# Prologue of an attention and mixture-of-experts kernel, written out per engine: constants in order of use, first key parts on VectorE

## What is computed

```python
x = x + xattn(layernorm(x), ctx, mask, mask, Wq, bq, Wk, bk, Wv, bv)
    # q, k, v = W @ . + b ; dot = q.k / 4 ; dot = mask*dot - (1-mask)*1e6
    # amap = softmax(dot) * mask ; out = amap.v
x = x + ffn(layernorm(x), gate_w, w1, w2)
    # top 2 of 8 experts: silu(x.w1g) * (x.w1u), then w2, weighted sum
```

## Time and profile before

| what | value |
|---|---|
| median of 3 runs | 975.49 us (974.23 to 975.64) |
| the profiled execution's own time | 971.9 us |
| its span, first to last instruction | 970.1 us |
| mean granted clock of PE | 0.937 of full speed |
| PE busy | 820.0 us (85%) |
| DVE, ACT, POOL busy | 547.9, 316.5, 377.2 us |

### The profile page before, as it was taken

The page is one execution under the profiler, slowest core; times in us unless marked ns, Lnnn a source line. Parts: engine busy times, 40 slices in busy tenths (PEclk is TensorE's granted clock), DMA queues, the critical chain, the costliest instruction groups (busy, mean ns, idle before and its releaser), DMA issues. The chain is left out here.

```text
span 970.1 us, 12844 instructions
## 1 busy us (share of the span) xinstructions
PE 820.0 (85%) x3737; PEld 366.6 (38%) x3738; DVE 547.9 (56%) x1055; ACT 316.5 (33%) x615; POOL 377.2 (39%) x396
## 2 busy tenths in 40 slices
PE   2078999999988998999899986159999999999994
PEld 1022323333333332333333322135555555555552
DVE  3186878788878877878788852403223232323322
ACT  0003556455545655555566675000000000000000
POOL 5643445457545754755474232401111111111111
PEclk9577999899999999999999998569999999999998
DMA  4553656566756856646664423322535365352332
GB/s 118 173 166 110 190 171 193 182 201 195 224 164 185 254 168 189 219 146 184 185 185 139 134 81 120 130 66 55 150 58 146 64 152 141 68 150 59 65 57 40
DMA packets 83567, 137.69 MB, mean 142 GB/s; under 512 B 13880, under 2 KB 39800, under 8 KB 83520
## 3 DMA queue, kind: packets, MB, share of 16 engines
q1 hardware_dynamic: 67792, 107.97, 36.7%
q0 software_dynamic: 7744, 17.86, 9.4%
q10 hardware_dynamic: 7984, 11.28, 4.0%
HBM read 77.34 MB, written 59.36 MB: 141 GB/s over the span
## 5 line engine op out<-in xcount | busy, mean ns | idle before, releaser
L731 DVE TENSOR_REDUCE mx<-tile 128x2 f32<-128x1024 f32 x256 | 309.0, 1217 | 67.8 <-PE tile L1005 64.8
L629 ACT ACTIVATE pr<-sc 128x512 f32<-128x512 f32 x512 | 268.8, 602 | 212.4 <-PE sc L992 209.5
L1005 PE MATMUL tile<-qk 97*128 97x512 bf16 x512 | 160.6, 397 | 43.8 <-DMA qk<-mrow_d 22.3
L1305 POOL DMA_INDIRECT out_dram<-y,ids x36 | 56.1, 1558 | 282.5 <-DVE ids L1230 278.4
L992 PE MATMUL sc<-qk 100*128 100x512 bf16 x512 | 156.2, 386 | 5.0 <-ACT pr L629 3.4
L1021 PE MATMUL pvb<-pr,vp 128*32 128x512 f32 x1024 | 141.3, 625 | 0.0
L1355 PE MATMUL dp<-wring,at 128*128 (+1 forms) x216 | 102.2, 609 | 13.4 <-DVE at L1240 13.4
L1285 ACT ACTIVATE sg<-gp 128x352 f32<-128x352 f32 x36 | 16.7, 463 | 291.7 <-PE up L1334 291.7
L1005 PEld LDWEIGHTS tile<-qk 97*128 97x128 bf16 x512 | 36.6, 98 | 182.5 <-DVE mx L731 75.9
L554 POOL TENSOR_SCALAR parts<-qkf 128x512 bf16<-128x512 f32 x32 | 48.3, 1511 | 140.5 <-DVE qkf L827 139.4
L1334 PE MATMUL gp<-wring,xtile 128*128 x288 | 94.0, 470 | 2.1 <-DVE meta L1221 2.1
(11 more groups left out here) (120 smaller groups left out, 742.2 us busy)
## 6 DMA issues: line engine op xcount, KB each, us to landing
qk<-stack_d SPq DMA_DIRECT2D x32, 768.0 KB
stack_d<-parts SPq DMA_DIRECT2D x32, 384.0 KB, 2.6
wring<-w_dram SPq DMA_DIRECT2D x32, 352.0 KB, 7.0
xl<-routed_d ACTq DMA_DIRECT2D x38, 257.0 KB, 2.7
stack_d<-parts SPq DMA_DIRECT2D x32, 256.0 KB, 2.9
pv_d<-ov SPq DMA_DIRECT2D x32, 256.0 KB, 3.5
xin<-x_dram SPq DMA_DIRECT2D x16, 256.0 KB, 5.8
cin<-ctxt_dram SPq DMA_DIRECT2D x8, 512.0 KB, 6.2
```

The costliest lines, as they stand in the source:

```text
L629: nc.scalar.activation(pr[s % 2][:, j, :], sc[(32 * u + 4 * s + j) % NSC][:, :], ACT.Exp, scale=SCALE).then_inc(exped.sem, 1)
L731: dve.tensor_reduce(mx[:, half(w), 2 * j:2 * j + 2], t[:, :, :], X, ALU.max, negate=True).then_inc(drained.sem, 1)
L1005: last = nc.tensor.matmul(t[:, i, :], qs[half(w)][0:RAW_ROWS, h, c * P:c * P + P], ks[half(w)][0:RAW_ROWS, h, :], start=True, stop=True)
L1305: pool.indirect_dma_start(out, bass.IndirectOffsetOnAxis(ap=ids[:, k, :], axis=0), y[:, k, :], None, compute_op=ALU.add).then_inc(y_added, 16)
```

## The change

Each engine's loop now starts at step -1; what steps -5 to -2 did is written out ahead of it.

- ACT issues `io`, `wq`, `bq`, `wk`, `bk` and `mask` first, with semaphores of their own (`io_in`, `wq_in`, `wk_in`, `mask_in`), and then the other seven.
- POOL sets the ones of half 0, waits for `io` alone, makes the deviations of two units, sets the ones of half 1, and makes the first query parts, two more deviations and the second query parts. It no longer makes the first key parts.
- DVE makes the first key parts itself in `key_parts`: a reduction with the maximum over groups of one element, a subtraction, such a reduction, a subtraction. It takes the statistics of two units before it normalises both; the copies of `idf` and `utf`, which need all the constants, come after the key parts.
- PE waits for `wq` or `wk` before a projection and for `const_made` and the ones only before the first raw scores.
- SP writes `mrow_d` before the query parts and does not wait for it until `stack(0, 0)`; both halves of unit 0 are read back one right after the other; the padding is written after step 1.

```diff
+        early = ((io[:, :], iotas, io_in),
+                 (wq_s[:, :, :], wq.rearrange("(c p) o -> p c o", p=P), wq_in),
+                 (bqk[:, 0, :], bq, wq_in),
+                 (wk_s[:, :, :], wk.rearrange("(c p) o -> p c o", p=P), wk_in),
+                 (bqk[:, 1, :], bk, wk_in),
+                 (mall[:, :], mask, mask_in))
...
 # SP
-            for u in range(FIRST, -2):
-                unit(u)
-
-            sp.wait_ge(const_made, MADE)
-            sp.wait_ge(ones_made, 4)
+            load_x(-5)
+            load_x(-4)
+            load_ctx(-3)
+            sp.wait_ge(mask_made, 2)
             for side in range(2):
                 sp.dma_start(mrow_d[:, side], mrow[:, side:side + 1, :].broadcast_to([B, 4, T])
                              ).then_inc(mrow_kept, 16)
+            load_x(-3)
+            load_x(-2)
+            keep_split(-3, 0)
+            keep_split(-2, 1)
             sp.wait_ge(mrow_kept, 32)
-            for i in range(4):
...
-            for u in range(-2, LAST + 1):
+            sp.wait_ge(ones_made, 1)
+            sp.wait_ge(split_kept[0].sem, split_kept[0].at(-3, "k"))
+            sp.wait_ge(split_kept[1].sem, split_kept[1].at(-2, "k"))
+            stack(0, 0)
+            stack(0, 1)
+            keep_split(-2, 0)
+            for u in range(-1, LAST + 1):
                 unit(u)
+                if u == 1:
+                    sp.wait_ge(const_made, MADE)
+                    pads()
 # POOL
-            for u in range(FIRST, LAST + 1):
+            ones_of(0)
+            pool.wait_ge(io_in, 16)
+            batch_rstd(-5)
+            batch_rstd(-4)
+            pool.wait_ge(rstd.sem, rstd.at(-4, "pow"))
+            ones_of(1)
+            part(-3, 0)
+            batch_rstd(-3)
+            batch_rstd(-2)
+            part(-2, 0)
+            for u in range(-1, LAST + 1):
 # DVE
+            def key_parts(u):
+                w = u + 2
+                src = qkf[:, half(w), 1, :]
...
+                dve.tensor_reduce(parts[:, 1, 0, :], src.rearrange("p (t o) -> p t o", o=1), X, ALU.max
+                                  ).then_inc(split[1].sem, 1)
...
+                dve.tensor_tensor(rest[:, 1, :], src, parts[:, 1, 0, :], ALU.subtract).then_inc(split[1].sem, 1)
...
+            for u in (-5, -4):
+                batch_stats(u, 0)
+                batch_stats(u, 1)
+            normalize(-5)
+            normalize(-4)
+            dve.wait_ge(mask_in, 16)
...
+            dve.wait_ge(wq_in, 32)
+            projection_out(-3, 0)
+            dve.wait_ge(wk_in, 32)
+            projection_out(-3, 1)
+            dve.wait_ge(const_made, MADE - 2)
+            key_parts(-2)
+            dve.wait_ge(const_loaded, CONST)
...
 # PE
-            pe.wait_ge(const_made, MADE)
-            pe.wait_ge(ones_made, 4)
+            pe.wait_ge(wq_in, 32)
+            project(-3, 0)
+            pe.wait_ge(wk_in, 32)
+            project(-3, 1)
+            project(-2, 0)
+            pe.wait_ge(const_made, MADE)
+            pe.wait_ge(ones_made, 4)
+            raw_scores(-2, 0)
...
```

More of the change, by code:

```diff
@@ L255, in attention @@
         pvb = st.enter_context(nc.psum_tensor("pvb", [P, T], F32))
+        io_in = sem("io_in")
+        mask_in = sem("mask_in")
+        wq_in = sem("wq_in")
+        wk_in = sem("wk_in")
         const_loaded = sem("const_loaded")
         const_made = sem("const_made")
+        mask_made = sem("mask_made")
         mrow_kept = sem("mrow_kept")
@@ L306, in attention @@
         block = st.enter_context(nc.Block())
-        const = ((idf[:, :], ident),
[L308 to L313, removed]
+        early = ((io[:, :], iotas, io_in),
[4 more added lines that the diff above has]
+                 (mall[:, :], mask, mask_in))
+        const = ((idf[:, :], ident),
                  (wv_s[:, :, :], wv.rearrange("(c p) o -> p c o", p=P)),
@@ L320, in attention @@
         CONST = 16 * len(const)
-        MADE = 9
+        MADE = 7
         @block.sync
@@ L419, in unit @@
             def unit(u):
-                if has(u + 1):
+                if has(u) and has(u + 1):
                     stack(u + 1, 1)
@@ L456, in unit, with pads @@
                                  mxt[:, :]).then_inc(maxrows.sem, 16)
-            for u in range(FIRST, -2):
-                unit(u)
-            sp.wait_ge(const_made, MADE)
-            sp.wait_ge(ones_made, 4)
+            def pads():
+                for i in range(4):
+                    sp.dma_start(routed_d[E * CAP + i * P:E * CAP + (i + 1) * P, :], pad[:, :]
+                                 ).then_inc(padded, 16)
+                sp.dma_start(out[TOKENS:TOKENS + P, :], pad[:, 0:T]).then_inc(padded, 16)
+            load_x(-5)
+            load_x(-4)
+            load_ctx(-3)
+            sp.wait_ge(mask_made, 2)
             for side in range(2):
@@ L484, in _, with ones_of @@
         def _(pool):
-            for h in range(2):
+            def ones_of(h):
                 pool.memset(ks[h][96:128, :, :], 1.0).then_inc(ones_made, 1)
@@ L489, in _ @@
                 pool.wait_ge(ones_made, 2 * h + 2)
-            pool.wait_ge(const_loaded, CONST)
             def values_out(u):
                 w = u + 1
+                pool.wait_ge(const_loaded, CONST)
                 pool.wait_ge(drained.sem, drained.at(u, "v"))
@@ L638, in unit @@
                         gate_weight(u)
+            for dst, src, loaded in early:
+                act.dma_start(dst, src).then_inc(loaded, 16)
             for dst, src in const:
@@ L944, in plan_tiles @@
                 do(dve.tensor_scalar(pairi[:, 3:4], pairi[:, 2:3], 1.0, None, ALU.subtract))
-            unit(FIRST)
+            def key_parts(u):
+                w = u + 2
+                src = qkf[:, half(w), 1, :]
+                dve.wait_ge(drained.sem, drained.at(u - 1, "k"))
+                dve.tensor_reduce(parts[:, 1, 0, :], src.rearrange("p (t o) -> p t o", o=1), X, ALU.max
+                                  ).then_inc(split[1].sem, 1)
+                dve.wait_ge(split[1].sem, split[1].at(u, 0))
+                dve.tensor_tensor(rest[:, 1, :], src, parts[:, 1, 0, :], ALU.subtract).then_inc(split[1].sem, 1)
+                dve.wait_ge(split[1].sem, split[1].at(u, 1))
+                dve.tensor_reduce(parts[:, 1, 1, :], rest[:, 1, :].rearrange("p (t o) -> p t o", o=1), X, ALU.max
+                                  ).then_inc(split[1].sem, 1)
+                dve.wait_ge(split[1].sem, split[1].at(u, 2))
+                dve.tensor_tensor(parts[:, 1, 2, :], rest[:, 1, :], parts[:, 1, 1, :], ALU.subtract
+                                  ).then_inc(split[1].sem, 1)
             dve.memset(pad[:, 0:T + 1], 0.0).then_inc(const_made, 1)
@@ L949, in _ @@
             dve.memset(before[:, :], 0.0).then_inc(const_made, 1)
-            dve.wait_ge(const_loaded, CONST)
+            for u in (-5, -4):
[4 more added lines that the diff above has]
+            dve.wait_ge(mask_in, 16)
+            dve.tensor_copy(mrow[:, 0, :], mall[:, :]).then_inc(mask_made, 1)
+            dve.tensor_scalar(mrow[:, 1, :], mall[:, :], 1.0, NEG / SCALE, ALU.subtract, ALU.mult
+                              ).then_inc(mask_made, 1)
+            dve.wait_ge(io_in, 16)
             dve.tensor_copy(first[:, :], io[0:1, 16:24]).then_inc(const_made, 1)
@@ L953, in _ @@
                               ).then_inc(const_made, 1)
+            dve.wait_ge(wq_in, 32)
[5 more added lines that the diff above has]
+            dve.wait_ge(const_loaded, CONST)
             dve.tensor_copy(idb[:, :], idf[:, :]).then_inc(const_made, 1)
             dve.tensor_copy(upper[:, :], utf[:, :]).then_inc(const_made, 1)
-            dve.tensor_copy(mrow[:, 0, :], mall[:, :]).then_inc(const_made, 1)
-            dve.tensor_scalar(mrow[:, 1, :], mall[:, :], 1.0, NEG / SCALE, ALU.subtract, ALU.mult
-                              ).then_inc(const_made, 1)
             dve.wait_ge(const_made, MADE)
-            for u in range(FIRST + 1, LAST + 1):
+            for u in (-3, -2):
+                batch_stats(u, 0)
+                batch_stats(u, 1)
+            normalize(-3)
+            projection_out(-2, 0)
+            normalize(-2)
+            for j in range(LEAD):
+                maximum(-2, j)
+            projection_out(-2, 1)
+            for u in range(-1, LAST + 1):
                 unit(u)
@@ L1126, in unit @@
                         project(u, 1)
-            for u in range(FIRST, LAST + 1):
+            pe.wait_ge(wq_in, 32)
[6 more added lines that the diff above has]
+            raw_scores(-2, 0)
+            raw_scores(-2, 1)
+            raw_scores(-2, 2)
+            raw_scores(-2, 3)
+            project(-2, 1)
+            for u in range(-1, LAST + 1):
                 unit(u)
```

3 lines of the change are left out of this document (removed).

## The result

The change makes the kernel faster by 1.5%: 957.91 us (956.78 to 958.49, 4 runs) against 974.86 (971.15 to 975.64, 4 runs), a ratio of 0.9849 with a 95% interval of 0.9817 to 0.988. The forecast was 960.4 in a range of 955.5 to 966.

What follows compares the result with a forecast made beforehand. PE was taken as busy to the end once raw scores start, so the prologue bounds: 10.34 plus 7.25 saved, together 17.6, less 2.5 for collisions, is 15.1, from median 975.5 to 960.4 us, range 955.5 to 966.

Steps and rivals of the forecast that it cites:

- the memset goes first: Rival: POOL's 3.51 memset beats DVE's second norm, norm 3.5 late, mask rows' 1.3 falls away; 962.6 us, chance 0.10.
- the rival without collisions: Rival: DVE and POOL do not hold each other in the prologue; 17.6 us saved, 957.9 us, chance 0.12.
- Start to the first projection: Step 1, kernel start until PE's first projection: from 17.83 to 7.49, 10.34 us earlier before collisions.
- First projection to the store of the query parts: Step 2, PE, DVE and POOL work unchanged; store moves from 27.99 to 17.65, adding nothing to the gain.
- The second collision: DVE's mask rows waiting behind POOL's second memset of ones, delaying the first copy: 0 to 1.3 us, taken as 1.3.
- The third: Collision of DVE's key-part subtractions with POOL's four query-part instructions: 0 to 2 x 0.75 us, taken as 0.95.
- Store to read: Step 3, store of the query parts to the read of the stack: 6.2 in place of 13.45, saving 7.25 us.
- The read of the stack: Step 4, read to first raw scores: stays 5.58 us; sharing with the second half taken as 0, bounds 0 to 2.8.
- What was costed at nothing: Includes key parts on DVE, 2.6 to 3.2 us, cover 2.6 or more; padding's 3.8 delay of a later read, slack 6.1.
- slower, one-element groups: Rival: reductions in `key_parts` cost by the group, holding DVE, store and PE; about 983 us at 25 ns a group, chance 0.03.
- Given back later: Rival: another clock fall plus padding's 3 or the shared read's 2.8 shrink the gain to some 10; 965 us, chance 0.10.
- Never reaches the end: Rival: something not on the prologue's chain sets the pace and the time stays at 975 us; chance 0.03.

Runs made afterwards that it cites:

- c0: The changed kernel run again with no edit; ratio 0.9852 to the kernel before, median 955.2 us against 969.7.
- e1: The changed kernel, with POOL waiting for the second norm, not the second deviation, before setting the ones of half 1; ratio 0.9855 to the kernel before.
- e2: The changed kernel, with the ones of half 1 set after the first query parts; median 953.4 us, ratio 0.9839 to the kernel before.
- e6: As e2, but the second half of unit 0 is read back only after the second query parts are stored; ratio 0.9798 to the kernel before.
- e3: The changed kernel, with the first key parts back on POOL behind the first query parts; median 961.4 us, ratio 0.99 to the kernel before.
- e4: The changed kernel, with the padding back between the stores of the query and the key parts; 969.6 us, one run.
- e8: The kernel before the change, with only the padding moved to after step 1; 964.7 us, one run.
- e5: The changed kernel, with the padding written after step 14 instead of step 1; 958.2 us, one run.

## Why the prediction was right, and where its steps were off

The kind and the direction came out: the start of the raw scores moves, and the end moves with it. The size lies in the range partly by luck. PE's timeline shows 13.1 saved ahead of the raw scores where the forecast had 15.1; the rival "the memset goes first" had 12.9, and that is what happened in the prologue. Its time was 962.6, and yet the median came out 2.5 under the forecast, at the very 957.9 of the rival without collisions, although the norm did collide. What made up the difference, 4.5 in all, is not in the forecast's sum and may be scatter: 1.1 in the rest of the kernel, and 3.4 because the profiled execution of before lay further under its median than that of the change. The second pair of medians (c0) differs by 14.5 and not by 17.0. By the steps:

1. *Start to the first projection*: 10.34 without collisions, 10.1 with the first of them. Measured 7.00. This is the step that failed, at the collision of the norm with the memset, and it failed by the rival "the memset goes first", which had a chance of 0.10. The argument was that DVE starts 0.04 after POOL's deviation and POOL only 0.09 after. The deviation ended at 6.83, DVE's norm began 0.04 later, at 6.87, and the memset 0.06 later, at 6.89. DVE was first by the record, and lost all the same. The small collision (POOL's second deviation) was 0.15, for which I had taken 0.25. e1 and e2 show that the memset is the cause, since the norm takes 0.55 again when it is moved, in e2 at the very same time. One line of before could have misled: its memset of 0.74 to 4.25 ran beside DVE's statistics at 3.65, which took their usual 0.69.

```profile
0.74 3.51 POOL L486 MEMSET qk<- 32x4096 bf16 x1 [0.29 <-POOLq L1412]
```

A smaller miss lay hidden under the long norm: without it PE waits for `bq` until 7.98 in e2 and 7.90 in e6, where the norm would let it start near 7.6.

2. *First projection to the store of the query parts*: taken as unchanged. 10.39 against 10.16 before: 0.28 more on PE, 0.19 less on POOL, the rest in gaps. The second collision, mask rows behind the memset, priced 1.3, cost nothing in this kernel, since the norm had already waited for the memset; e1 shows it where the norm does not: the copy came 0.75 after PE's tile. The third, the key parts, priced 0.95, was 0 to 0.3 (e3).
3. *Store to read*: 13.45 to 6.2 forecast, 6.08 measured. e4 and e8 give the padding 3.3 to 4.7 of it, e3 gives the key parts on DVE 3.5 to 3.9.
4. *The read of the stack*: taken as 5.58 with 0 to 2.8 as bounds; 6.64 measured. Taking 0 "as the first was issued first" was wrong, e6.

Added up: 7.00 less 0.23, plus 7.37, less 1.06, is the 13.08 that PE's timeline shows. I had 15.1. The norm made it 3.1 less and the read 1.1 less; the two later collisions, priced 2.25 together, made it 2.0 more, as they and all gaps came to 0.23. The rest of the kernel gave 1.1 more in this execution. That the median fell by 17.0 and not by 14.2 is none of it: the offset of 3.6 that I had carried from the profiled execution of before to its median was there in that kernel's runs (3.0 with the fourth run) and not in the changed one's (0.2).

What was costed at nothing: the key parts at 2.6 to 3.2 took 3.3 and finished at 21.74, 0.5 after POOL's query parts, while SP was still issuing the query parts' store (to about 22.8). The cover was 1.1 and not 2.6, because the second projection was slow for longer (3.11, starting at 14.37, against 1.88 from 21.14). That is a matter of the execution: in c0, the same kernel, the second projection took 1.88, the key parts ended at 20.08, and the cover was 2.7 (22.8 less 20.08). The padding: the read behind it was issued at 132.08 and first used at 141.02, 8.9 and not 11.7 later, and PE waited 0.26. The delay of 3.8 was mis-sized, and the slack a little. The padding made the issue 2.4 later (in the result the read was issued 3.40 after the transfer ahead of the padding, 128.68, and in e5, without padding, 0.97 after it). And the read took 8.8 to land (c0: issued 129.65, used 138.42, its weight load waiting for it) where the read before it, without padding ahead, takes 5.6 (result: issued 118.85, used 124.49), 3.2 more where I had taken 1.5. Together 5.6. The slack was 5.4 and not 6.1: without padding ahead (e5) the read is issued at 126.93 and used at 137.88, 10.95 later, of which landing takes 5.6. So the cover was used up: in c0 only the weight load waited, in the result a matmul too, by 0.26.

The other rivals: *slower, one-element groups* fell with the first line of L982, 0.69 for 512 groups of one, the same as the subtraction or the statistics over 512 elements. *Given back later* did not happen: the padding cost 0.26 (e5), and the clock fell about as often after as before: of 143 stretches of 4 us from the first raw scores on, 20 have a granted clock under 0.8, and 19 before. *Never reaches the end*: the start of the raw scores and the end of the routing move together, 47.02 and 620.92 before, 33.94 and 606.87 after.

The rule cited from the Trainium skill ("SBUF — State Buffer", section "Who interferes with whom") was right in the main: a norm beside a memset was held for the whole of it, which no row of before could show. With the whole memset at stake, 0.10 was too little for a lead of 0.05. Two points of the rule are not borne out by these traces. It gives the port to the one that issues first, and the record has DVE first by 0.02; either the recorded start is not the moment that decides, or the rule is not so, and no run here tells which. And it lets two inputs in SBUF on DVE exclude every POOL instruction that reads SBUF (a condition that the prediction's sentence left out): L990, from 20.60, was indeed held by POOL's two-input L581, which ended at 21.20 (it took 1.14 in place of 0.69), but L985 took its usual 0.69 at 19.15, in the midst of POOL's one-input L578 (18.46 to 19.96).

## What to carry to other kernels

A prologue in front of an engine that is busy to the end was worth nearly its full length here (13.1 of 14.2), and it was made of waits that were wider than their need: a semaphore for all constants, cleanup writes ahead of the critical read, a fill of a buffer for the second unit ahead of the first one's work. When you move a long POOL fill, look at what DVE wants at its start and put the fill behind the next hand-over, not at the same event: e2 and e6 do that, and their raw scores start 2.2 to 4.0 earlier than with the change. And take the time of a fixed milestone (here the first raw scores) from the profile when totals of the same kernel spread by more than the edit.

## What was not expected of the hardware

- A DVE instruction that was recorded 0.02 to 0.03 us ahead of a POOL memset of 3.51 was held until 0.27 to 0.28 after the memset's end, in five profiles of five. In this case the order of the recorded starts did not tell who runs.
- The memset only writes, to 32 partitions, and holds DVE's norm and casts all the same (e1: 2.35 for a cast of 0.41). It did not hold DVE's statistics (0.69 at 3.65 in the trace of before).
- DVE's subtraction with two inputs in SBUF runs at full speed beside a POOL instruction with one input and waits for the end of one with two (1.40 in e1, where L985 starts at 15.41 and L575 ends at 16.26). In c0 it then slows the next of POOL's: L985 takes 0.94 from 17.68, across the end of L575 at 18.09, and L578, starting at 18.17, takes 1.81 in place of 1.50.

```profile
17.68 0.94 DVE L985 TENSOR_TENSOR rest<-qkf,parts 128x512 f32<-128x512 f32 x1
```
```profile
16.93 1.16 POOL L575 TENSOR_TENSOR rest<-qkf,parts 128x512 f32<-128x512 f32 x1
18.17 1.81 POOL L578 TENSOR_SCALAR parts<-rest 128x512 bf16<-128x512 f32 x1
```

- Two reads of 768 KB on one queue, 1.1 us apart, do not follow one another: the first takes about 1 us longer (5.5 to 6.0 without the second, 6.5 to 7.4 with it), not twice its time.
- PE's first projection took 3.35 to 3.78 for what takes 1.88 later, and how far the slow rate reached into the second one differed (3.11 in the result, 1.88 in c0) between executions of the same kernel. The rows give a granted clock of 1.00 for that whole stretch (11 to 19 in the result), so this slowness does not show in them as the later falls do (0.50 from 28 to 55 in the trace of before).
